# The experts' down projection as three fp32r products instead of one fp32 product, with the operands split by ScalarE and VectorE

## The chip, the cores and the metric

The kernel runs on one core of a Trainium2 chip. The metric is the device time of one execution in microseconds (us), taken as the median of several runs. TensorE does matmuls, transposes and weight loads; VectorE (DVE), ScalarE (ACT) and GpSimd (POOL) do elementwise work; SyncE (SP) only issues DMAs here. Each engine works through its own instructions in order, and semaphores tie the engines together.

## The reference

One layer over 1024 tokens (32 sequences of 32) of width 512, in fp32: `x + cross_attention(layernorm(x))`, then `x + delta_rule_attention(layernorm(x))`, then `x + mixture_of_experts(layernorm(x))`. Only the last part is touched. Every token goes to 2 of 8 experts, and an expert is

```python
gate = jnp.einsum('bted,edf->btef', dispatched, gate_proj)   # 512 -> 1408
up = jnp.einsum('bted,edf->btef', dispatched, up_proj)       # 512 -> 1408
acts = jax.nn.silu(gate) * up
expert_out = jnp.einsum('btef,efd->bted', acts, down_proj)   # 1408 -> 512
```

summed over the two experts with the routing weights.

## The kernel before

The kernel runs its stages one after another. The last, `experts`, works on tokens that `route` has sorted by expert into 23 tiles (`TILES`) of 128 rows. A tile is cut along the 1408 hidden columns into six blocks (`NB`): blocks 0 to 4 are 256 columns wide, block 5 is 128 wide. One step `n` is one block of one tile, so there are 138 steps; `b = n % 6` is the block and `s = n // 6` the tile. "A full block" below is one of 256 columns, "the half block" is block 5.

All weights of the current expert lie in SBUF, gate and up in `w_gu`, down in `w_d`. SyncE reloads them in three groups of two blocks, only where the expert changes (`cond=fresh`), each group once the tile before has done with it. `load_down` waits for that in front of the next loads in the same queue.

What the engines do with a block:

- **The split.** ScalarE copies a block of gate and up weights (128x2048) into fp32r, `gh` (L1495); VectorE subtracts that from the weights and gets the remainder `gl` (L1548). The ring of four buffers lets ScalarE do block n+3 and VectorE block n+2 in step n. The tokens are split likewise once a tile (`xh` L1479, `xl` L1539).
- **gate_up(n)**, TensorE: 12 fp32r matmuls, three products `gh·xh`, `gl·xh`, `gh·xl` for each of four slices (L1437 to L1439), into PSUM.
- **silu** by ScalarE (L1508), times the up half by VectorE, giving `hid` (L1562).
- **turn_h(n)**: TensorE transposes `hid` (L1447), ScalarE copies it from PSUM to `hT` (L1519).
- **down(n)**: TensorE multiplies `hT` with `w_d` in plain fp32 (L1460), one product for each chunk of 128 hidden columns: two chunks in a full block, one in the half block. All 11 chunks of a tile add up in one PSUM bank. ScalarE stores the result at the end (`store_y`, L1485, L1487).

The order on the engines is written out by hand. In step n it is, on TensorE: `gate_up(n)`, `down(n - 2)`, `turn_h(n - 1)`, and `turn_x` for the next tile if `b == 2`. On ScalarE: silu(n); `store_y` of the last tile if `b == 1`; the copy `gh(n + 3)`; the copy `hT(n - 1)`; `take_x` if `b == 2`. On VectorE: hid(n), gl(n + 2), and `split_x` if `b == 2`. `hid`, `silu` and `hT` each have two buffers.

Of the kernel before, what the change touches and what calls it, by code (L numbers as in the profile page):

```python
# [11 lines left out]
F32 = mybir.dt.float32  # L12
F32R = mybir.dt.float32r
U8 = mybir.dt.uint8
I32 = mybir.dt.int32
ALU = mybir.AluOpType
# [3 lines left out]
P = 128  # L20
B, N, C = 32, 32, 512
# [22 lines left out]
BLK = 256  # L44
RING = 4
NB = -(-F // BLK)
# [1303 lines left out]
def experts(nc, d, ps, ident, x_nat, slot, slot_w, tile_expert, out):  # L1350


    with ExitStack() as ctx:
        sb = lambda name, shape, dt=F32: ctx.enter_context(nc.sbuf_tensor(name, shape, dt))
        sem = lambda name: ctx.enter_context(nc.semaphore(name))
        w_gu, w_d = sb("w_gu", [P, KC, 2, F]), sb("w_d", [P, FC, C])
# [2 lines left out]
        gh, gl = ([sb(f"{name}{i}", [P, KC, 2, BLK], F32R) for i in range(RING)] for name in ("gh", "gl"))  # L1359
        silu = [sb(f"silu{i}", [P, BLK]) for i in range(2)]  # L1360
        hid = [sb(f"hid{i}", [P, BLK]) for i in range(2)]
        hT = [sb(f"hT{i}", [P, BLK // P, P]) for i in range(2)]
        y = [sb(f"y{i}", [P, C]) for i in range(2)]
        spare = w_gu[:, :, :, :].rearrange("p k a f -> p (k a f)")
        yg = [[spare[:, (2 * t + r) * C:(2 * t + r + 1) * C] for t in range(NT)] for r in range(2)]
# [11 lines left out]
        with nc.Block() as block:  # L1377
            @block.sync
            def _(sp):
                def load_x(s):  # L1380
                    if s >= 3:
                        sp.wait_ge(x_turned, s - 2)
                    sp.dma_start(xs[s % 3][:, :], d["x_slots"][s * P:(s + 1) * P, :]).then_inc(x_in[s % 3], 16)

                def load_gate_up(s, e, g):
                    if s:
                        sp.wait_ge(gl_done, (s - 1) * NB + 2 * g + 2)
                    cols = group(g)
                    for n, src in enumerate(("gate_proj", "up_proj")):
                        sp.dma_start(w_gu[:, :, n, cols],  # L1390
                                     d[src][bass.ds(e, 1), :, cols].rearrange("a (k p) f -> p (a k) f", p=P), cond=fresh).then_inc(gu_in[g], 16)

                def load_down(s, e, g):
                    if s:
                        sp.wait_ge(d_done, (s - 1) * NB + 2 * g + 2)
                    rows = group(g)
                    sp.dma_start(w_d[:, rows.start // P:rows.stop // P, :],
                                 d["down_proj"][bass.ds(e, 1), rows, :].rearrange("a (c p) n -> p (a c) n", p=P), cond=fresh).then_inc(d_in[g], 16)

                load_x(0)  # L1400
                for s in range(TILES):
                    e = sp.value_load(tile_expert[0:1, 0, s:s + 1], min_val=0, max_val=E - 1)
                    fresh = sp.value_load(tile_expert[0:1, 1, s:s + 1], min_val=0, max_val=1)
                    if s + 1 < TILES:
                        load_x(s + 1)
                    load_gate_up(s, e, 0)
                    load_gate_up(s, e, 1)
                    load_down(s, e, 0)
                    load_gate_up(s, e, 2)
                    load_down(s, e, 1)  # L1410
                    load_down(s, e, 2)
                for t in range(NT):
                    sp.wait_ge(summed, 2 * (t + 1))
                    sp.dma_start(out.rearrange("b n c -> (b n) c")[t * P:(t + 1) * P, :], x_nat[:, t, :]).then_inc(stored, 16)
                sp.wait_ge(stored, 16 * NT)

            @block.tensor
            def _(pe):
                def turn_x(s):
                    pe.wait_ge(x_in[s % 3], 16 * (s // 3 + 1))  # L1420
                    if s:
                        pe.wait_ge(xl_done, s)
                    for k in range(KC):
                        mm = pe.transpose(ps[X_BANK][:, k * P:(k + 1) * P], xs[s % 3][:, k * P:(k + 1) * P], ident[:, :])  # L1424
                    mm.then_inc(x_turned, 1)

                def gate_up(n):
                    s, b, bw = n // NB, n % NB, width(n % NB)
                    if b == 0:
                        pe.wait_ge(xl_done, s + 1)  # L1430
                    pe.wait_ge(gl_done, n + 1)
                    if n >= 3:
                        pe.wait_ge(hid_done, n - 2)
                    bank = ps[GU_BANK + n % 3][:, 0:2 * bw].rearrange("p (a f) -> p a f", a=2)
                    for k in range(KC):
                        hi, lo = gh[n % RING][:, k, :, 0:bw], gl[n % RING][:, k, :, 0:bw]
                        pe.matmul(bank, xh[s % 2][:, k, :], hi, start=(k == 0), stop=False)  # L1437
                        pe.matmul(bank, xh[s % 2][:, k, :], lo, start=False, stop=False)  # L1438
                        mm = pe.matmul(bank, xl[s % 2][:, k, :], hi, start=False, stop=(k == KC - 1))  # L1439
                    mm.then_inc(gu_done, 1)  # L1440

                def turn_h(n):
                    pe.wait_ge(hid_done, n + 1)
                    if n >= 2:
                        pe.wait_ge(hT_done, n - 1)
                    for c in range(width(n % NB) // P):
                        mm = pe.transpose(ps[H_BANK + n % 2][:, c * P:(c + 1) * P], hid[n % 2][:, c * P:(c + 1) * P], ident[:, :])  # L1447
                    mm.then_inc(h_turned, 1)

                def down(n):  # L1450
                    s, b = n // NB, n % NB
                    pe.wait_ge(hT_done, n + 1)
                    if b % 2 == 0:
                        pe.wait_ge(d_in[b // 2], 16 * (s + 1))
                    if b == 0 and s >= 2:
                        pe.wait_ge(y_ready, s - 1)
                    cs = range(width(b) // P)
                    bank = ps[Y_BANK + s % 2]
                    for c in cs:
                        mm = pe.matmul(bank, hT[n % 2][:, c, :], w_d[:, b * (BLK // P) + c, :], start=(b == 0 and c == 0),  # L1460
                                       stop=(b == NB - 1 and c == cs[-1]))
                    mm.then_inc(d_done, 1)

                turn_x(0)
                for n in range(STEPS + 2):
                    if n < STEPS:
                        gate_up(n)
                    if n >= 2:
                        down(n - 2)
                    if 1 <= n <= STEPS:  # L1470
                        turn_h(n - 1)
                    if n % NB == 2 and n // NB + 1 < TILES:
                        turn_x(n // NB + 1)

            @block.scalar
            def _(act):
# [12 lines left out]
                def split_gate_up(n):  # L1489
# [3 lines left out]
                    if n >= RING:  # L1493
                        act.wait_ge(gu_done, n - RING + 1)
                    nc.scalar.copy(gh[n % RING][:, :, :, 0:bw].rearrange("p k a f -> p (k a) f"),  # L1495
                                   w_gu[:, :, :, b * BLK:b * BLK + bw].rearrange("p k a f -> p (k a) f")).then_inc(gh_done, 1)

                split_gate_up(0)
                take_x(0)
                split_gate_up(1)  # L1500
                split_gate_up(2)
                for n in range(STEPS + 2):
                    if n < STEPS:
                        bw = width(n % NB)
                        act.wait_ge(gu_done, n + 1)
                        if n >= 2:
                            act.wait_ge(hid_done, n - 1)
                        nc.scalar.activation(silu[n % 2][:, 0:bw], ps[GU_BANK + n % 3][:, 0:bw], ACT.Silu).then_inc(silu_done, 1)  # L1508
                    if n >= 2 and (n - 2) % NB == NB - 1:
                        store_y((n - 2) // NB)  # L1510
                    if n + 3 < STEPS:
                        split_gate_up(n + 3)
                    if 1 <= n <= STEPS:
                        m = n - 1
                        bw = width(m % NB)
                        act.wait_ge(h_turned, m + 1)
                        if m >= 2:
                            act.wait_ge(d_done, m - 1)
                        nc.scalar.copy(hT[m % 2][:, 0:bw // P, :].rearrange("p c n -> p (c n)"),  # L1519
                                       ps[H_BANK + m % 2][:, 0:bw]).then_inc(hT_done, 1)  # L1520
                    if n % NB == 2 and n // NB + 1 < TILES:
                        take_x(n // NB + 1)

# [12 lines left out]
            def _(dve):  # L1536
# [6 lines left out]
                def split_gate_up(n):  # L1543
                    b, bw = n % NB, width(n % NB)
                    dve.wait_ge(gh_done, n + 1)
                    if n >= RING:
# [3 lines left out]
                                            gh[n % RING][:, :, :, 0:bw].rearrange("p k a f -> p (k a) f").bitcast(F32),  # L1550
                                            ALU.subtract).then_inc(gl_done, 1)

                split_gate_up(0)
                split_x(0)
                split_gate_up(1)
                for n in range(STEPS + 1):
                    if n < STEPS:
                        bw = width(n % NB)
                        dve.wait_ge(silu_done, n + 1)
# [3 lines left out]
                                                ALU.mult).then_inc(hid_done, 1)  # L1563
                    if n + 2 < STEPS:
                        split_gate_up(n + 2)
                    if n % NB == 2 and n // NB + 1 < TILES:
                        split_x(n // NB + 1)
                for t in range(NT):
# [64 lines left out]
```

## Time and profile before

| | |
|---|---|
| median of 3 runs | 2028.21 us (2022.68 to 2029.91) |
| the profiled execution: own time | 2025.16 us |
| the profiled execution: span | 2023.4 us |
| mean granted TensorE clock, as a share of 2.4 GHz | 0.892 |
| TensorE matmul busy | 1584.4 us, 78% |
| VectorE busy | 1183.8 us, 59% |
| ScalarE busy | 707.2 us, 35% |
| the 506 instructions of the down projection (L1460) | 242.2 us of TensorE |

The span is the time from the first to the last instruction; the own time is what the run is counted with. Busy shares are means over stages that have different limits, so they say little about one stage. A matmul's duration runs from its start until its results are through the array; matmuls overlap, so what one costs in a stream is the distance between two starts and not the duration. The same holds, less strongly, for neighbouring instructions of VectorE and ScalarE.

### The profile page before, as it was taken

Reading aid. Unit: us, or ns where it says so; the run is one execution under the profiler, and the core shown is the slowest. Engines: PE = TensorE matmul, PEld = TensorE weight load, DVE = VectorE, ACT = ScalarE, POOL = GpSimd, SP = SyncE. Lnnn points to the kernel's source line nnn. Section 1 sums busy time; section 2 is a strip of 40 time slices with the busy share of each in tenths; the row PEclk is TensorE's granted clock in tenths of the full one; section 3 lists DMA queues with packets and bytes.
Section 4 is the critical chain, followed back from the end, with each engine's and each line's share of the span. In section 5 each row is a group of like instructions: output and inputs, shape, how many; then the busy total and the mean of one; then the engine's idle time right before and its main releaser. Section 6 shows DMA issues by size and latency. Waiting matters only on the chain. (4 is left out here: it accounts for less than half of the span.)

```text
span 2023.4 us, 21832 instructions
## 1 busy us (share of the span) xinstructions
PE 1584.4 (78%) x7119; PEld 1126.2 (56%) x7119; DVE 1183.8 (59%) x2547; ACT 707.2 (35%) x1358; POOL 90.2 (4%) x262
## 2 busy tenths in 40 slices
PE   6999999999599999309600079609999999999993
PEld 3777777777477777203200056406666666666662
DVE  3355545654503888999999733225555555555553
ACT  2333333333234554200000112105555555555550
POOL 0000000000000000002111100030000000000003
PEclk9999999999799999759855579759999999999997
DMA  3111011100125335513000142045435515325004
GB/s 110 33 32 31 16 31 31 31 22 10 39 90 88 71 44 62 88 48 114 0 0 0 41 125 47 1 175 197 161 133 183 176 37 192 130 84 192 22 11 130
DMA packets 116487, 153.31 MB, mean 76 GB/s; under 512 B 47120, under 2 KB 68112, under 8 KB 116400
## 3 DMA queue, kind: packets, MB, share of 16 engines
q1 hardware_dynamic: 110528, 137.81, 23.3%
q0 software_dynamic: 2560, 8.39, 1.3%
q10 hardware_dynamic: 3312, 6.03, 0.8%
q8 instruction: 44, 0.72, 0.2%
q14 instruction: 43, 0.35, 0.1%
HBM read 250.58 MB, written 31.39 MB: 139 GB/s over the span
## 5 line engine op out<-in xcount | busy, mean ns | idle before, releaser
L1548 DVE TENSOR_TENSOR gl<-w_gu,gh 128x2048 fp32r<-128x2048 f32 x138 | 290.8, 2107 | 34.3 <-ACT gh L1495 34.3
L1495 ACT CAST gh<-w_gu 128x2048 fp32r<-128x2048 f32 x138 | 242.4, 1757 | 66.3 <-DMA w_gu<-in_up_proj 56.4
L1460 PE MATMUL bank<-w_d,hT 128*128 128x512 f32 x506 | 242.2, 597 | 9.4 <-ACT hT L1519 9.3
L1437 PE MATMUL bank<-gh,xh 128*128 128x512 f32 (+1 forms) x552 | 219.3, 397 | 11.6 <-DVE xl L1539 11.4
L1562 DVE TENSOR_TENSOR hid<-silu,bank 128x256 f32<-128x256 f32 x138 | 55.1, 399 | 263.6 <-ACT silu L1508 263.5
L1439 PE MATMUL bank<-gh,xl 128*128 128x512 f32 (+1 forms) x552 | 207.4, 376 | 0.0
L1438 PE MATMUL bank<-gl,xh 128*128 128x512 f32 (+1 forms) x552 | 206.5, 374 | 0.0
L1113 PE MATMUL bank<-o_v,o_outw 128*128 128x64 f32 x256 | 36.3, 311 | 182.6 <-DMA o_v<-scratch_v_rows 182.6
L1113 PEld LDWEIGHTS bank<-o_v,o_outw 128*128 128x128 f32 x256 | 36.2, 227 | 186.5 <-DMA o_v<-scratch_v_rows 183.6
L1460 PEld LDWEIGHTS bank<-w_d,hT 128*128 128x128 f32 x506 | 91.6, 188 | 82.8 <-issue 55.2
L939 PE MATMUL bank<-wg,xnT 128*128 128x512 f32 x128 | 61.5, 625 | 88.1 <-DMA bg_row<-in_bg 88.1
L1508 ACT ACTIVATE silu<-bank 128x256 f32<-128x256 f32 x138 | 50.7, 367 | 216.6 <-PE bank L1439 216.6
L1437 PEld LDWEIGHTS bank<-gh,xh 128*128 128x128 f32 x552 | 104.3, 189 | 33.3 <-DVE xl L1539 11.8
L497 DVE COPY probT<-bank 128x512 f32<-128x512 f32 x64 | 41.1, 685 | 134.1 <-PE bank L385 134.1
L1439 PEld LDWEIGHTS bank<-gh,xl 128*128 128x128 f32 x552 | 104.1, 189 | 20.3
L1438 PEld LDWEIGHTS bank<-gl,xh 128*128 128x128 f32 x552 | 104.7, 190 | 15.5
L947 ACT ACTIVATE r_root<-r_nm 128x8 f32<-128x8 f32 x32 | 6.7, 210 | 281.9 <-DVE r_nm L1025 281.9
L939 PEld LDWEIGHTS bank<-wg,xnT 128*128 128x128 f32 x128 | 23.9, 197 | 124.1 <-DMA bg_row<-in_bg 88.3
L449 ACT ACTIVATE prob<-bank,neg_max 128x257 f32<-128x257 f32 x128 | 59.1, 474 | 78.2 <-DVE neg_max L484 78.2
L995 DVE TENSOR_TENSOR r_prod<-r_gram,r_pr 128x512 f32<-128x512 f32 (+23 forms) x158 | 83.8, 549 | 0.0
L436 ACT COPY xv<-bank 128x512 f32<-128x512 f32 x64 | 37.6, 588 | 125.4 <-PE bank L345 125.4
L343 PE MATMUL bank<-xa_wkv_hi,ctx_hi 128*128 128x512 f32 x192 | 78.6, 409 | 0.6 <-PEq L240 0.6
(256 smaller groups left out, 3028.5 us busy)
## 6 DMA issues: line engine op xcount, KB each, us to landing
w_gu<-in_gate_proj SPq DMA_DIRECT2D x46, 1024.0 KB
w_gu<-in_up_proj SPq DMA_DIRECT2D x46, 1024.0 KB
w_d<-in_down_proj SPq DMA_DIRECT2D x46, 1024.0 KB
w_gu<-in_gate_proj SPq DMA_DIRECT2D x23, 768.0 KB
w_gu<-in_up_proj SPq DMA_DIRECT2D x23, 768.0 KB
w_d<-in_down_proj SPq DMA_DIRECT2D x23, 768.0 KB
ctx_raw<-in_ctxT SPq DMA_DIRECT2D x32, 385.5 KB, 3.9
scratch_gram<-gram SPq DMA_DIRECT2D x8, 768.0 KB, 3.3
```

What stands on the lines that cost most here:

```text
L343: pe.matmul(bank, hi(k), other_hi(k), start=(k == 0), stop=False)
L449: nc.scalar.activation(prob[s][:, c, :], ps[c][:, 0:M], ACT.Exp, bias=neg_max[s][:, c:c + 1], accum_out=total[s][:, c:c + 1]).then_inc(exp ...
L939: pe.matmul(ps[n % 8], xnT[:, k, t * P:(t + 1) * P], wg[:, k, hf * 512:(hf + 1) * 512], start=(k == 0), stop=False)
L995: ins = tt(parts[x][:, a], G[:, :, lo:hi, 2, 0:cols], bc(pr[nxt % 2][:, a, :, None, 0:cols], [SG, hi - lo, cols]), ALU.mult)
L1113: mm = pe.matmul(ps[O_BANK + 2 * s + h // 8][:, (h % 8) * DK:(h % 8 + 1) * DK], outw[s][:, h, :], v_row[s][:, h, :], start=True, stop=True)
L1437: pe.matmul(bank, xh[s % 2][:, k, :], hi, start=(k == 0), stop=False)
L1438: pe.matmul(bank, xh[s % 2][:, k, :], lo, start=False, stop=False)
L1439: mm = pe.matmul(bank, xl[s % 2][:, k, :], hi, start=False, stop=(k == KC - 1))
L1460: mm = pe.matmul(bank, hT[n % 2][:, c, :], w_d[:, b * (BLK // P) + c, :], start=(b == 0 and c == 0), stop=(b == NB - 1 and c == cs[-1]))
L1495: nc.scalar.copy(gh[n % RING][:, :, :, 0:bw].rearrange("p k a f -> p (k a) f"), w_gu[:, :, :, b * BLK:b * BLK + bw].rearrange("p k a f -> ...
L1548: nc.vector.tensor_tensor(gl[n % RING][:, :, :, 0:bw].rearrange("p k a f -> p (k a) f"), w_gu[:, :, :, b * BLK:b * BLK + bw].rearrange("p ...
L1562: nc.vector.tensor_tensor(hid[n % 2][:, 0:bw], silu[n % 2][:, 0:bw], ps[GU_BANK + n % 3][:, bw:2 * bw], ALU.mult).then_inc(hid_done, 1)
```

## The change

The down projection becomes three fp32r products like those of gate and up. For a block, `hh` is the fp32r copy of the transposed hidden block and `hl` what remains; `dh` and `dl` are the same for the block of down weights. TensorE then does `hh·dh`, `hh·dl` and `hl·dh` for each chunk. ScalarE makes `hh` (in the place of `hT`) and then `dh`; VectorE makes `hl` and `dl` in step n + 1, behind its other work of that step. Each of the four has two buffers. The wait for the down weights' arrival moves from TensorE to ScalarE, and SyncE's reload of `w_d` waits for `dl` instead of for the down projection. `hT_done` now says that `hh` is there.

```diff
-        hT = [sb(f"hT{i}", [P, BLK // P, P]) for i in range(2)]
+        hh, hl = ([sb(f"{name}{i}", [P, BLK // P, P], F32R) for i in range(2)] for name in ("hh", "hl"))
+        dh, dl = ([sb(f"{name}{i}", [P, BLK // P, C], F32R) for i in range(2)] for name in ("dh", "dl"))
+        hl_done, dh_done, dl_done = sem("hl_done"), sem("dh_done"), sem("dl_done")
...
                 def load_down(s, e, g):
                     if s:
-                        sp.wait_ge(d_done, (s - 1) * NB + 2 * g + 2)
+                        sp.wait_ge(dl_done, (s - 1) * NB + 2 * g + 2)
...
                 def turn_h(n):
                     pe.wait_ge(hid_done, n + 1)
                     if n >= 2:
-                        pe.wait_ge(hT_done, n - 1)
+                        pe.wait_ge(hl_done, n - 1)
...
                 def down(n):
                     s, b = n // NB, n % NB
-                    pe.wait_ge(hT_done, n + 1)
-                    if b % 2 == 0:
-                        pe.wait_ge(d_in[b // 2], 16 * (s + 1))
+                    pe.wait_ge(hl_done, n + 1)
+                    pe.wait_ge(dl_done, n + 1)
...
                     for c in cs:
-                        mm = pe.matmul(bank, hT[n % 2][:, c, :], w_d[:, b * (BLK // P) + c, :], start=(b == 0 and c == 0),
-                                       stop=(b == NB - 1 and c == cs[-1]))
+                        pe.matmul(bank, hh[n % 2][:, c, :], dh[n % 2][:, c, :], start=(b == 0 and c == 0), stop=False)
+                        pe.matmul(bank, hh[n % 2][:, c, :], dl[n % 2][:, c, :], start=False, stop=False)
+                        mm = pe.matmul(bank, hl[n % 2][:, c, :], dh[n % 2][:, c, :], start=False, stop=(b == NB - 1 and c == cs[-1]))
                     mm.then_inc(d_done, 1)
...
+                def split_down(n):                                     # ScalarE
+                    s, b, cs = n // NB, n % NB, width(n % NB) // P
+                    if b % 2 == 0:
+                        act.wait_ge(d_in[b // 2], 16 * (s + 1))
+                    if n >= 2:
+                        act.wait_ge(d_done, n - 1)
+                    nc.scalar.copy(dh[n % 2][:, 0:cs, :], w_d[:, b * (BLK // P):b * (BLK // P) + cs, :]).then_inc(dh_done, 1)
...
-                        nc.scalar.copy(hT[m % 2][:, 0:bw // P, :].rearrange("p c n -> p (c n)"),
+                        nc.scalar.copy(hh[m % 2][:, 0:bw // P, :].rearrange("p c n -> p (c n)"),
                                        ps[H_BANK + m % 2][:, 0:bw]).then_inc(hT_done, 1)
+                        split_down(m)
...
+                def split_down(n):                                     # VectorE
+                    b, cs = n % NB, width(n % NB) // P
+                    if n >= 2:
+                        dve.wait_ge(d_done, n - 1)
+                    dve.wait_ge(hT_done, n + 1)
+                    nc.vector.tensor_tensor(hl[n % 2][:, 0:cs, :].rearrange("p c n -> p (c n)"), ps[H_BANK + n % 2][:, 0:cs * P],
+                                            hh[n % 2][:, 0:cs, :].rearrange("p c n -> p (c n)").bitcast(F32), ALU.subtract).then_inc(hl_done, 1)
+                    dve.wait_ge(dh_done, n + 1)
+                    nc.vector.tensor_tensor(dl[n % 2][:, 0:cs, :], w_d[:, b * (BLK // P):b * (BLK // P) + cs, :],
+                                            dh[n % 2][:, 0:cs, :].bitcast(F32), ALU.subtract).then_inc(dl_done, 1)
...
                 split_gate_up(0)
                 split_x(0)
                 split_gate_up(1)
-                for n in range(STEPS + 1):
+                for n in range(STEPS + 2):
...
                     if n + 2 < STEPS:
                         split_gate_up(n + 2)
+                    if 1 <= n <= STEPS:
+                        split_down(n - 1)
                     if n % NB == 2 and n // NB + 1 < TILES:
                         split_x(n // NB + 1)
```

## Rows read from the trace of the kernel before

**Rows 1.** Windows: length; PE, PEld, DVE, ACT, POOL busy (count); clock, DMA share, GB/s.

```profile
1864.17:1891.14 26.97, 26.63 (x110) 18.14 (x110) 15.23 (x13) 14.91 (x21) 0.00 (x0) 1.00 0.15 55
1390.09:1984.96 594.87, 586.29 (x2396) 398.54 (x2395) 332.15 (x284) 325.05 (x437) 0.00 (x0) 1.00 0.35 121
```

**Rows 2.** Timeline of TensorE over that tile: start, duration, instruction, idle before.

```profile
1864.17 1.98 PE L1460 MATMUL bank<-w_d,hT 128*128 128x512 f32 x4 [0.34 <-ACT hT L1519]
...
1869.41 1.88 PE L1460 MATMUL bank<-w_d,hT 128*128 128x512 f32 x4
1871.13 0.38 PE L1447 MATMUL bank<-ident,hid 128*128 128x128 f32 x2
...
1871.59 0.40 PE L1438 MATMUL bank<-gl,xh 128*128 128x512 f32 x1
...
1874.13 1.88 PE L1460 MATMUL bank<-w_d,hT 128*128 128x512 f32 x4
...
1877.51 1.88 PE L1460 MATMUL bank<-w_d,hT 128*128 128x512 f32 x4
...
1882.21 1.88 PE L1460 MATMUL bank<-w_d,hT 128*128 128x512 f32 x4
...
1886.81 1.02 PE L1460 MATMUL bank<-w_d,hT 128*128 128x512 f32 x2
...
1890.41 0.39 PE L1439 MATMUL bank<-gh,xl 128*128 128x512 f32 x1
1891.14 1.98 PE L1460 MATMUL bank<-w_d,hT 128*128 128x512 f32 x4 [0.34 <-ACT hT L1519]
```

**Rows 3.** Timeline of ScalarE over the same tile.

```profile
1864.29 1.04 ACT L1495 CAST gh<-w_gu 128x1024 fp32r<-128x1024 f32 x1
1866.41 0.37 ACT L1519 COPY hT<-bank 128x256 f32<-128x256 f32 x1 [1.07 <-PE bank L1447]
...
1869.61 0.39 ACT L1508 ACTIVATE silu<-bank 128x256 f32<-128x256 f32 x1 [2.18 <-PE bank L1439]
1869.89 1.90 ACT L1495 CAST gh<-w_gu 128x2048 fp32r<-128x2048 f32 x1
...
1887.86 0.59 ACT L1485 COPY y<-bank 128x512 f32<-128x512 f32 x1 [0.47 <-PE bank L1460]
...
1888.91 1.92 ACT L1495 CAST gh<-w_gu 128x2048 fp32r<-128x2048 f32 x1 [0.45 <-ACT y L1485]
1890.73 0.36 ACT L1519 COPY hT<-bank 128x256 f32<-128x256 f32 x1
```

**Rows 4.** Timeline of VectorE over the same tile.

```profile
1867.46 0.69 DVE L1539 TENSOR_TENSOR xl<-bank,xh 128x512 fp32r<-128x512 f32 x1 [0.41 <-ACT xh L1479]
1870.03 0.42 DVE L1562 TENSOR_TENSOR hid<-silu,bank 128x256 f32<-128x256 f32 x1 [1.87 <-ACT silu L1508]
1870.37 1.22 DVE L1548 TENSOR_TENSOR gl<-w_gu,gh 128x1024 fp32r<-128x1024 f32 x1
...
1875.09 2.28 DVE L1548 TENSOR_TENSOR gl<-w_gu,gh 128x2048 fp32r<-128x2048 f32 x1
```

**Rows 5.** Timeline of ScalarE where the expert has changed.

```profile
1412.16 1.91 ACT L1495 CAST gh<-w_gu 128x2048 fp32r<-128x2048 f32 x1 [2.63 <-DMA w_gu<-in_up_proj]
```

**Rows 6.** Timeline of TensorE at the end of the stage.

```profile
1984.96 1.88 PE L1460 MATMUL bank<-w_d,hT 128*128 128x512 f32 x4
...
1989.97 1.13 PE L1460 MATMUL bank<-w_d,hT 128*128 128x512 f32 x2 [0.35 <-ACT hT L1519]
```

**Rows 7.** Timeline of TensorE before the experts' stage.

```profile
1275.29 1.09 PE L1123 MATMUL bank<-ident,o_g 128*128 128x128 f32 x8 [2.21 <-DVE o_g L1204]
```

**Rows 8.** Windows, busy time and granted clock around it.

```profile
1260.00:1280.00 20.00, 16.34 (x74) 9.81 (x73) 6.57 (x9) 3.82 (x7) 0.00 (x0) 1.00 0.00 0
```

**Rows 9.** Timeline of TensorE in the stage's first step, at the lower clock.

```profile
1366.90 0.63 PE L1438 MATMUL bank<-gl,xh 128*128 128x512 f32 x1
1367.33 0.63 PE L1439 MATMUL bank<-gh,xl 128*128 128x512 f32 x1
```

## The prediction

> **What bounds the kernel now.** I began with the page. Its slices show the experts' stage as the last third of the span, with TensorE at nine tenths or more. Then I measured one tile by windows: 26.97 us, of which TensorE is busy 26.63, VectorE 15.23 and ScalarE 14.91, at full clock [rows 1]. So TensorE sets the pace, and VectorE has 11.7 us a tile to spare and ScalarE 12.1. The shares stop there: they don't say whether new work of those two will be finished in time for TensorE. For that I read the timelines of the three engines over this tile.
>
> The reader should mark in the timeline of TensorE the moments when gate_up(n) is through and down(n-2) may start. I call them E, with the block b of step n as number: E3 = 1869.41, E4 = 1874.13, E5 = 1877.51, E0 = 1882.21, E1 = 1886.81 [rows 2]. In step b=2 the last gate-and-up matmul starts at 1890.41. Such matmuls follow one another every 0.23 us (1871.59 to 1874.13 is 11 of them), so E2 is 1890.64; the down projection starts at 1891.14. That is the one wait of the tile, 0.50 us, and its first weight load then isn't hidden: the group takes 1.98 instead of 1.88 us, 0.10 more [rows 2].
>
> The cause is the useful find. In step b=1 ScalarE stores y before it copies `gh`, so the copy of `hT` comes late: y at E1 + 1.05, `gh` at E1 + 2.10, `hT` at E1 + 3.92, done at E1 + 4.28 [rows 3]. In an ordinary step ScalarE starts silu at E + 0.20 and `gh` at E + 0.48, and a successor starts 0.10 us before the duration ends (1888.91 + 1.92 against 1890.73), so `hT` starts at E + 2.28 [rows 3]. TensorE wants it at the next step's E, over 3 us later in most steps.
>
> **The gain on TensorE.** Two chunks cost 1869.41 to 1871.13, 1.72 us, 0.86 a chunk [rows 2]. Three fp32r products cost 3 x 0.23 = 0.69 a chunk. That saves 0.17 a chunk: 0.34 in a full block, 0.17 in the half one, 11 x 0.17 = 1.87 us a tile. The stretches between the E's without waits, old and new, are: E2 to E3 (with turn_x) 5.14, 4.80; E3 to E4 4.72, 4.38; E4 to E5 3.38, 3.04; E5 to E0 4.70, 4.36; E0 to E1 4.60, 4.26; E1 to E2 (its down projection is the half block) 3.83, 3.66. New sum: 24.50 us.
>
> **The work added.** For a full block: `hh` costs what `hT` does, 0.37. `dh` is 128x1024 on ScalarE, like the half `gh`: 1.04 [rows 3]. `hl` reads PSUM at 256 columns like `hid`: 0.42. `dl` is 128x1024 on VectorE, like the half `gl`: 1.22 [rows 4]. For the half block: `dh` 0.62 (1.04 less 512 columns at the 0.84 ns that two sizes of `gh`, 1.90 and 1.04, give), `hl` 0.29, `dl` 0.69 like `xl` [rows 4]. VectorE rises to 15.23 + 5 x 1.64 + 0.98 = 24.4 us a tile, ScalarE to 14.91 + 5 x 1.04 + 0.62 = 20.7. Both are just under 24.5: by throughput all is hidden. By order it isn't.
>
> The row and the Trainium skill differ here on one price. "VectorE: DVE Perf Modes", section on the TRN2 errata, gives SBUF-source operations 58 cycles beside one per element at 0.96 GHz, so an estimated 1.13 us for `dl`; the row with 1.22 is this very shape. By the page the three large waits below would each shrink by 0.09, some 6 us in all.
>
> **The chain.** down(n-1) now needs `dl(n-1)`, the last thing that VectorE does in step n, behind `hid`, `gl(n+2)` and `hl`, and behind `dh(n-1)`, the last thing of ScalarE in that step. In an ordinary full step: ScalarE has `hh` at E + 2.28, `dh` from E + 2.56 to E + 3.60. VectorE starts `hid` at E + 0.62 and `gl` 0.34 later [rows 3, 4], which leaves it at E + 3.16, and does `hl` until E + 3.50. `dl` waits for `dh`: E + 3.63 to E + 4.85. With 0.05 us until TensorE starts (`hT` 1890.73 + 0.36 to 1891.14), down(n-1) can start at E + 4.90. TensorE gets there at 4.38 or sooner. Step by step through the tile; each line is the step in which `dl` is made, the wait falls at the next E, and 0.10 is for the exposed load at a wait:
>
> - b=0: the half block's `dl` is ready at E0 + 4.1, TensorE comes at 4.26: no wait.
> - b=1: the down projection of three matmuls ends 0.16 earlier, so y starts at E1 + 0.89, `gh` at 1.94, `hh` at 3.76, `dh` 4.04 to 5.08, `dl` 5.11 to 6.33, ready 6.38. TensorE comes at E1 + 3.66. **Wait 2.72**, with the load 2.82.
> - b=2: TensorE is late itself now. turn_h(n-1) starts at E2 + 2.82 + 1.38 = 4.20, and `hh` 0.42 later (1866.41 against a transpose started at about 1865.99, that is 1864.17 + 1.82), so `dl` is ready at 7.24; TensorE comes at 2.82 + 4.80 = 7.62: no wait.
> - b=3: the ordinary case, 4.90 against 4.38: wait 0.52, with load 0.61.
> - b=4: turn_h is later by that 0.61, `hh` at E4 + 2.41, ready at 5.03; TensorE comes at 0.61 + 3.04 = 3.65 (gate_up is the half block): wait 1.38, with load 1.48.
> - b=5: `hh` at E5 + 1.48 + 1.38 + 0.42 = 3.28, ready 5.90; TensorE comes at 5.84: wait 0.06, with load 0.16.
>
> Sum: 5.07 us of waits, a tile of 24.50 + 5.07 = 29.57 us, 2.60 more than 26.97. Over the 22 tile-to-tile periods: **+57.2 us**.
>
> **The rest.** The first tile stores no y. Its ordinary waits cost some 1.2 us more than it saves. At the end nothing covers the chain: today the last gate_up is through at 1984.96 and the last down projection ends at 1991.10, 6.1 later [rows 6]. New, from the same point: wait 1.3 for `dl`, 0.10 + 1.38 until turn_h, 0.42, then 2.62 (`hh` 0.28, `dh` 1.04, `dl` 1.22 and 0.08 between) gives 5.9; again 1.48, 0.3, and 1.6 for the half block gives 9.2; 0.9 of matmuls: 10.1. That is +4.0; the last tile's shorter steps give 0.5 back: **+3.5**. Down weights: ScalarE asks for them some 2 us before TensorE did, and SyncE reloads them about 1.4 us earlier; with a tile between reload and use that moves nothing. Gate and up: at a change of expert ScalarE waits up to 2.63 us for `w_gu` [rows 5], in step b=3. SyncE sends that load behind the wait for the half block's `w_d`, which now ends with its `dl` about 1.1 us earlier, while b=3 comes 4 us later after E1 (3.66 + 7.62 against 3.83 + 0.50 + 5.24 = 9.57, so 1.7, in all 2.8): the wait vanishes. The 22 tiles took 594.87 us, 1.5 more than 22 x 26.97 [rows 1], so **-1.5**, no more.
>
> Sum: 57.2 + 1.2 + 3.5 - 1.5 = +60.4 on 2025.16, so 2085.6. The profiled execution was 3.05 below the median of its runs; I forecast **2088 us**, 3.0% slower.
>
> **The rivals.**
>
> 1. *The forecast, 0.72.* For it: each duration has a row of its own shape, and the 0.50 us wait shows the chain of b=1 at work already.
> 2. *Throughput decides, 0.07.* Waits shrink because what is late in one step is caught up in the next; TensorE's 24.50 then counts beside today's wait of 0.6. 22 x (25.10 - 26.97) = -41, near 1987 us. It wins if the waits sum to under 2.47 us a tile. Against it: `dl` stands behind `gl` in VectorE's order, and nothing lets it pass.
> 3. *Only the y wait is real, 0.07.* If the small instructions run about 0.5 us shorter in sum, b=3 and half of b=4 fall away: 24.50 + 2.82 makes +0.35 a tile, +8, and the end +3: near 2038. Slightly longer b=4 waits lead up to 2060.
> 4. *The clock falls, 0.10.* TensorE would stand idle about 2.5 us in each tile. The longest such gap that I find at full clock is 2.21 us, in a stretch where it was 82% busy and the clock stayed 1.00 [rows 7, 8]; mine would be just longer, at 83% busy. At the lower clock matmuls follow every 0.43 instead of 0.23 us [rows 9]. If the first 8 behind the wait ran so, 22 x 8 x 0.20 = +35: 2123. All 18 of that step: +79, of which later waits would absorb some. The Trainium skill ("TensorE: Matmul & The Clock Gate", Why this matters for your kernels) says likewise that idle gaps between bursts return the clock to half; no row of this case shows it for so short a gap.
> 5. *Other sizes, 0.04,* such as slower copies while DMAs run.
>
> **Range and chances.** An error of 0.2 us in each of three waits is 13 us. That gives 2062 to 2112 about the likeliest; the clock's first case takes the upper end to 2125, and about 2 in 10 stay out. Half a percent, 10 us, is about what a measurement can tell from no change. Faster 0.07; within it 0.05 (part of rival 3); slower 0.88.
>
> **What the profile after would show.** Right: L1460's place taken by 759 matmuls 0.23 us apart; a tile of about 29.6 us, TensorE idle 5 us of it; VectorE near 83% busy and ScalarE 70% in that stage; the wait of the first down matmul put down to VectorE's `dl`, 2.5 to 2.8 us once a tile in front of block 0's down projection, and 1.4 and 0.5 us in front of those of blocks 3 and 2; `dl` waiting for ScalarE's `dh`. Wrong: waits spread evenly or absent, `dl` starting well before E + 3.6, or a granted clock under 1.00 behind the long wait.

## The result, and the profile after

The changed kernel takes 2116.55 us (median of 4 runs, 2115.56 to 2116.89) against 2026.64 for the kernel before in the same runs: a ratio of 1.0444, 95% interval 1.0423 to 1.0464. It is 4.4% slower. The forecast was 2088, the range 2062 to 2125.

The page of the changed kernel, busy shares and the span in 40 slices:

```profile
PE 1578.3 (75%) x7372; PEld 1186.4 (56%) x7372; DVE 1383.2 (65%) x2823; ACT 829.3 (39%) x1496; POOL 89.7 (4%) x262
...
PE   6999999998799995077000796188888888888882
...
PEclk9999999999799998589555797599999999999996
```

TensorE is busy for 6 us less than before and the span is 92 us longer. In the experts' stage its slices read eight where they read nine. VectorE's busy time has grown by 199 us and ScalarE's by 122.

The windows of two tiles, from one store of y to the next. Columns as in [rows 1]:

```profile
1682.22:1713.38 31.16, 26.76 (x123) 21.05 (x121) 23.92 (x26) 20.29 (x26) 0.00 (x0) 0.95 0.06 18
1713.38:1743.24 29.86, 25.43 (x123) 20.08 (x121) 23.83 (x26) 20.28 (x26) 0.00 (x0) 1.00 0.79 282
```

The second of these is a tile at full clock: 29.86 us against 26.97 [rows 1], with VectorE at 80% and ScalarE at 68%. The first takes 1.3 us more, and there the mean granted clock is 0.95. The 21 periods between two stores, the last left out, come in two kinds: nine of 29.80 to 29.87 us and twelve of 31.15 to 31.63.

The timeline of TensorE in the tile at full clock, with the end of the tile before it (the first three rows, where the clock is full again). L1461, L1462, L1463 are `hh·dh`, `hh·dl`, `hl·dh`; only marked starts are shown, to be read as [rows 2] were:

```profile
1703.55 0.47 PE L1461 MATMUL bank<-dh,hh 128*128 128x512 f32 x1 [1.34 <-DVE dl L1572]
...
1708.16 0.47 PE L1461 MATMUL bank<-dh,hh 128*128 128x512 f32 x1
...
1712.49 0.39 PE L1461 MATMUL bank<-dh,hh 128*128 128x512 f32 x1
...
1715.93 0.39 PE L1441 MATMUL bank<-gh,xl 128*128 128x512 f32 x1
1718.91 0.47 PE L1461 MATMUL bank<-dh,hh 128*128 128x512 f32 x1 [2.59 <-issue]
...
1723.80 0.39 PE L1461 MATMUL bank<-dh,hh 128*128 128x512 f32 x1
...
1728.80 0.47 PE L1461 MATMUL bank<-dh,hh 128*128 128x512 f32 x1 [0.49 <-DVE dl L1572]
...
1733.40 0.47 PE L1461 MATMUL bank<-dh,hh 128*128 128x512 f32 x1 [1.34 <-DVE dl L1572]
```

The last gate-and-up matmul of step b=2 starts at 1715.93, so E2 is 1716.16, and the down projection starts at 1718.91: a wait of 2.75 us. From 1723.80 to 1728.80 is the next: down(n-1) starts 5.00 us after E3. The forecast had 4.90. The profile names VectorE's `dl` as the one waited for, except at 1718.91, where it finds nobody; there the next rows show that it was `dl` too.

ScalarE and VectorE in step b=1 of the same tile, to be read as [rows 3, 4] were:

```profile
1713.38 0.59 ACT L1487 COPY y<-bank 128x512 f32<-128x512 f32 x1 [0.31 <-PE bank L1463]
...
1714.43 1.92 ACT L1497 CAST gh<-w_gu 128x2048 fp32r<-128x2048 f32 x1 [0.45 <-ACT y L1487]
1716.24 0.37 ACT L1529 CAST hh<-bank 128x256 fp32r<-128x256 f32 x1
1716.50 1.05 ACT L1506 CAST dh<-w_d 128x1024 fp32r<-128x1024 f32 x1
```

```profile
1716.71 0.42 DVE L1569 TENSOR_TENSOR hl<-bank,hh 128x256 fp32r<-128x256 f32 x1 [0.98 <-ACT hh L1529]
1717.58 1.22 DVE L1572 TENSOR_TENSOR dl<-w_d,dh 128x1024 fp32r<-128x1024 f32 x1 [0.45 <-ACT dh L1506]
```

y, then `gh`, then `hh`, then `dh`, and only then, at 1717.58, VectorE's `dl`, which ends at 1718.80. TensorE starts 0.11 us later. Here is the chain of the forecast, link by link: E1 is 1712.49, so y is at E1 + 0.89 (forecast 0.89), `gh` at 1.94 (1.94), `hh` at 3.75 (3.76), `dh` at 4.01 (4.04), `dl` at 5.09 (5.11) and the down projection at 6.42 (6.38).

The waits over the whole stage: who waited for whom, us in total, times, the longest:

```profile
DVE dl L1572 <- ACT dh L1506: 49.0, 115, 0.5
PE bank L1461 <- DVE dl L1572: 48.6, 48, 2.8
...
ACT gh L1497 <- DMA w_gu<-in_up_proj: 1.2, 1, 1.2
```

`dl` waits for `dh` in 115 of 138 steps, 0.4 us each time: the two helpers work one behind the other. ScalarE's waits for gate and up weights at a change of expert are gone: the one that is left, 1.2 us at 1369.31, belongs to the stage's first loads, and the kernel before has it too (1.24 us at 1366.85).

TensorE behind the long wait in the tile before (1682 to 1713):

```profile
1687.74 0.76 PE L1461 MATMUL bank<-dh,hh 128*128 128x512 f32 x1 [2.57 <-issue]
...
1689.16 0.63 PE L1461 MATMUL bank<-dh,hh 128*128 128x512 f32 x1
...
1690.44 0.50 PE L1449 MATMUL bank<-ident,hid 128*128 128x128 f32 x2
```

The gap was the same, 2.57 us, but here the matmuls take 0.63 to 0.76 instead of 0.39 to 0.47 us, and the two groups of three are 1.42 and 1.28 us apart instead of 0.77 and 0.69. That is the lower clock of rival 4.

### The profile page after: what moved, and what is told of

The parts are those of the page before. It is cut to its first block and busy times, and to the rows that moved or that the text cites. A ratio compares the mean times of both kernels' runs of the same rounds, so it can differ in the third digit from the quotient of the medians.

```text
span 2115.1 us, 23025 instructions
## 1 busy us (share of the span) xinstructions
PE 1578.3 (75%) x7372; PEld 1186.4 (56%) x7372; DVE 1383.2 (65%) x2823; ACT 829.3 (39%) x1496; POOL 89.7 (4%) x262
## 5 line engine op out<-in xcount | busy, mean ns | idle before, releaser
L1439 PE MATMUL bank<-gh,xh 128*128 128x512 f32 (+1 forms) x552 | 219.3, 397 | 12.8 <-DVE xl L1550 12.6
L1461 PE MATMUL bank<-dh,hh 128*128 128x512 f32 x253 | 113.2, 447 | 104.9 <-issue 54.3
L1572 DVE TENSOR_TENSOR dl<-w_d,dh 128x1024 fp32r<-128x1024 f32 x138 | 156.6, 1135 | 49.0 <-ACT dh L1506 49.0
L1506 ACT CAST dh<-w_d 128x1024 fp32r<-128x1024 f32 x138 | 135.6, 983 | 0.0
L1461 PEld LDWEIGHTS bank<-dh,hh 128*128 128x128 f32 x253 | 50.4, 199 | 144.1 <-issue 134.5
L1463 PE MATMUL bank<-dh,hl 128*128 128x512 f32 x253 | 106.3, 420 | 0.0
L1462 PE MATMUL bank<-dl,hh 128*128 128x512 f32 x253 | 105.7, 418 | 0.0
L1569 DVE TENSOR_TENSOR hl<-bank,hh 128x256 fp32r<-128x256 f32 x138 | 55.2, 400 | 61.1 <-ACT hh L1529 58.9
```

The source lines that it names most:

```text
L1461: pe.matmul(bank, hh[n % 2][:, c, :], dh[n % 2][:, c, :], start=(b == 0 and c == 0), stop=False)
L1462: pe.matmul(bank, hh[n % 2][:, c, :], dl[n % 2][:, c, :], start=False, stop=False)
L1463: mm = pe.matmul(bank, hl[n % 2][:, c, :], dh[n % 2][:, c, :], start=False, stop=(b == NB - 1 and c == cs[-1]))
L1506: nc.scalar.copy(dh[n % 2][:, 0:cs, :], w_d[:, b * (BLK // P):b * (BLK // P) + cs, :]).then_inc(dh_done, 1)
L1572: nc.vector.tensor_tensor(dl[n % 2][:, 0:cs, :], w_d[:, b * (BLK // P):b * (BLK // P) + cs, :], dh[n % 2][:, 0:cs, :].bitcast(F32), ALU.su ...
```

## The experiments

Times are medians, each with the ratio to the kernel before on the same chip. The rows come from different chips, on which the kernel before took 2024.97 to 2027.25 us, so differences of a few us between rows are better read from the ratios. A tile is the period between two stores of y in the profile.

| run | us | ratio, 95% interval | tile, us |
|---|---|---|---|
| the change | 2116.55 | 1.0444 (1.0423 to 1.0464) | 29.86 or 31.4 |
| filler matmuls in the long wait | 2095.07 | 1.0331 (1.0314 to 1.0348) | 29.85 |
| store of y late | 2073.82 | 1.0233 (1.0216 to 1.0250) | 28.40 |
| `dh`, `dl` a step earlier | 2010.21 | 0.9913 (0.9897 to 0.9930) | 26.28 |
| both of these | 1986.44 | 0.9800 (0.9784 to 0.9817) | 25.22 |
| down weights split only twice | 2012.42 | 0.9930 (0.9913 to 0.9946) | 26.28 |
| kernel before, store late | 2017.07 | 0.9952 (0.9936 to 0.9969) | 26.35 |
| both, `hh`/`hl` first in block 4 | 2008.11 | 0.9911 (0.9894 to 0.9927) | 26.27 |
| both, old condition for the reload | 2012.68 | 0.9943 (0.9924 to 0.9962) | 25.23, seven of 28.0 to 32.5 |
| the change, old condition for the reload | 2113.58 | 1.0438 (1.0421 to 1.0456) | 29.84 or 31.4, one 32.9 |

**Is it the clock that makes 12 of 21 tiles longer?**

```diff
                     if n < STEPS:
                         gate_up(n)
+                    if n % NB == 2 and n >= NB:
+                        for _ in range(8):
+                            pe.matmul(ps[X_BANK], xh[(n // NB) % 2][:, 0, :], gh[n % RING][:, 0, :, 0:BLK], start=True, stop=True)
                     if n >= 2:
                         down(n - 2)
```

> The changed kernel, and in every tile but the first TensorE does 8 needless fp32r matmuls into a PSUM bank that is free at that moment, in front of block 0's down projection, where it stands idle for 2.6 us; they take 8 x 0.23 = 1.84 us. In the changed kernel's trace 8 of the 22 periods between two stores of y take 29.8 to 29.9 us at full clock and 14 take 31.2 to 31.6 us, with the lower clock behind that wait. Theory A (the clock falls because of the idle stretch and costs the 1.5 us in these 14 tiles and at the end): all periods become 29.8 to 29.9 us, granted clock 1.00 in the stage, time down by 15 x 1.5 = 22 us to about 2094. Theory B (the longer tiles come from something else, such as loads of weights or late engines, and the lower clock only goes with it): the periods stay mixed and the time stays at 2115 to 2118. Theory C (the filler matmuls get in the way): above 2120.

(The counts in it are off: it is nine and twelve, and the last, longer period beside them.) Measured: 2095.07, as theory A said. TensorE around the fillers (L1472), and the window of 100 us, whose clock is now 1.00:

```profile
1736.27 1.98 PE L1472 MATMUL bank<-gh,xh 128*128 128x512 f32 x8
1739.00 0.47 PE L1461 MATMUL bank<-dh,hh 128*128 128x512 f32 x1 [0.76 <-issue]
1739.31 0.40 PE L1462 MATMUL bank<-dl,hh 128*128 128x512 f32 x1
```

```profile
1700.00:1800.00 100.00, 91.43 (x429) 72.42 (x428) 79.53 (x84) 67.50 (x88) 0.00 (x0) 1.00 0.36 123
```

All of the 21 periods but two are 29.8 to 29.9 us. In one of the two (30.55) the expert changes and ScalarE waits 0.63 us for `w_gu`; in the other (30.12) it doesn't change, and ScalarE's `gh` starts 0.28 us later behind y than in the other tiles. TensorE did 176 needless matmuls and the kernel became 21.5 us faster: what twelve longer tiles at 1.5 us and the longer end at 2.4 us had cost. So rival 4 is real, and it is one of two causes, not the only one: without it the kernel is still 3.3% slower than before.

**Is the long wait the store of y?**

```diff
-                    if n >= 2 and (n - 2) % NB == NB - 1:
-                        store_y((n - 2) // NB)
...
                     if n % NB == 2 and n // NB + 1 < TILES:
                         take_x(n // NB + 1)
+                    if n >= 2 and (n - 2) % NB == NB - 1:
+                        store_y((n - 2) // NB)
```

> The changed kernel, with ScalarE's store of y moved from behind silu to the end of its step; nothing else. Theory A (the long wait in front of block 0's down projection is the store in front of gh, hh and dh, and the clock falls only because of that wait): that wait goes from 2.6 to about 1.2 us, a tile takes 29.85 - 1.5 = 28.3 us, the clock stays at 1.00, time 2116 - 22 x 1.5 - 22 = 2061, range 2050 to 2070. Theory B (the chain of an ordinary step is all that matters and the store is beside the point): no shorter than 2105. Theory C (waits move: what block 0 gains is lost by block 1, whose copies now run behind the store): 2085 to 2100 with the clock at 1.00.

Measured 2073.82, tile 28.40, at full clock. The wait is 1.13 us where 1.2 was expected. The mechanism is theory A's, the time 13 us above it and beyond its range. The periods tell most of it: seven of them, those in which the expert changes, take 28.8 to 31.5 us, 10 us more than seven of 28.40. There ScalarE waits for `w_gu`, 1.60 us in this one, and TensorE in turn, 2.19 us, with the lower clock behind it (the matmul takes 0.67). So the clock didn't stay at 1.00 either: it fell in two of the seven.

```profile
1558.70 1.91 ACT L1497 CAST gh<-w_gu 128x2048 fp32r<-128x2048 f32 x1 [1.60 <-DMA w_gu<-in_up_proj]
```

```profile
1551.63 0.47 PE L1461 MATMUL bank<-dh,hh 128*128 128x512 f32 x1 [1.13 <-issue]
...
1563.22 0.67 PE L1461 MATMUL bank<-dh,hh 128*128 128x512 f32 x1 [2.19 <-DVE dl L1572]
...
1569.22 0.47 PE L1461 MATMUL bank<-dh,hh 128*128 128x512 f32 x1 [1.17 <-DVE dl L1572]
```

So the long wait had been giving the loads their time: with it ScalarE waits for `w_gu` at no change of expert, without it at all seven. I had not thought of that in the expectation, though the prediction counts it.

**Order or amount?**

```diff
-        dh, dl = ([sb(f"{name}{i}", [P, BLK // P, C], F32R) for i in range(2)] for name in ("dh", "dl"))
+        dh, dl = ([sb(f"{name}{i}", [P, BLK // P, C], F32R) for i in range(3)] for name in ("dh", "dl"))
...
-                        split_down(m)
+                    if n < STEPS:
+                        split_down(n)
...
                     if 1 <= n <= STEPS:
-                        split_down(n - 1)
+                        split_hidden(n - 1)
+                    if n < STEPS:
+                        split_down(n)
```

VectorE's `split_down` is cut in two (`split_hidden` makes `hl`), and `d_done` is asked for one step less strictly for `dh` and `dl`.

> The changed kernel, with dh and dl made one step earlier (three buffers each): in step n ScalarE makes dh(n) and VectorE dl(n), behind hh(n-1) and hl(n-1). The work of each engine is unchanged; only what down(n-1) waits for gets shorter, ending with hl(n-1). The store of y stays where it was. Theory A (order, not amount, costs the time): the waits in front of blocks 2, 3 and 4 vanish, the one of block 0 goes from 2.6 to about 1.0 us, a tile takes 24.5 + 1.1 = 25.6 us, time 2026 - 22 x 1.4 = 1996, range 1985 to 2010, faster than the kernel before. Theory B (the amount costs it: VectorE with 24.4 us a tile and ScalarE with 20.7 can't keep up, since each waits for the other): 2030 or more, with VectorE over 90% busy.

Measured 2010.21, tile 26.28 where theory A said 25.6: faster than the kernel before, just above the range that theory A gave. Theory B is out: the same work, on the same engines, costs 106 us less where TensorE doesn't wait for it, the clock's part included. Two waits are left in a tile:

```profile
1723.52 0.50 PE L1461 MATMUL bank<-dh,hh 128*128 128x512 f32 x1 [0.85 <-DVE hl L1570]
...
1736.42 0.50 PE L1461 MATMUL bank<-dh,hh 128*128 128x512 f32 x1 [0.45 <-DVE hl L1570]
```

0.85 in front of block 0 was expected as 1.0. The other, 0.45 in front of block 3, was not: I had written that it would vanish. `hl` stands behind `gl` in VectorE's order and is ready some 3.6 us after E4, while the next gate_up is the half block and takes TensorE there in 3.04.

> The changed kernel without the repeated split of the down weights: dh and dl are made for the first two blocks only and used for all later ones, so the down projection is computed with the wrong weights from block 2 on. TensorE does the same 759 matmuls; ScalarE is spared dh (5 x 1.05 + 0.63 us a tile), VectorE dl (5 x 1.22 + 0.68). What down(n-1) waits for ends with hl(n-1), as in the run with dh and dl one step earlier, whose tile took 26.28 us. Theory A (order): dh and dl cost nothing once they are not what TensorE waits for, so this kernel's tile takes the same 26.1 to 26.4 us and the time is 2005 to 2014. Theory B (amount): freed of a quarter of their work the engines are faster than in that run, a tile of 25.5 us or less, below 1998.

```diff
-                        split_down(m)
+                        if m < 2:
+                            split_down(m)
...
+                    if n >= 2:
+                        return
                     dve.wait_ge(dh_done, n + 1)
...
-                    pe.wait_ge(dl_done, n + 1)
+                    pe.wait_ge(dl_done, min(n, 1) + 1)
```

(The wait for `d_in` goes back to TensorE and the reload's condition to `d_done`.) Measured 2012.42, tile 26.28:

```profile
1700.00:1726.30 26.30, 25.00 (x123) 20.26 (x122) 17.25 (x20) 15.04 (x21) 0.00 (x0) 1.00 0.08 26
```

The same window of the run with `dh` and `dl` a step earlier:

```profile
1719.72:1746.01 26.29, 24.99 (x123) 20.24 (x121) 23.51 (x26) 20.13 (x27) 0.00 (x0) 1.00 0.12 34
```

VectorE does 17.25 instead of 23.51 us of work in that time, ScalarE 15.04 instead of 20.13, and the ordinary tile isn't 0.01 us shorter. The split of the down weights costs nothing once it is off the path. The tiles are the fair comparison here and not the times: with the old condition for the reload ScalarE waits for `w_gu` at all seven changes of expert, up to 2.55 us, and in the other run at none.

**Both edits, and the fair comparison.**

> Both of the last two edits: dh and dl one step earlier, and the store of y at the end of ScalarE's step. Theory A: no wait is left on TensorE but small ones, a tile takes 24.5 to 25.0 us, time 2026 - 22 x 2.2 = 1978, range 1968 to 1990. Theory B (VectorE's 24.4 us a tile is now the bound): a tile takes 25.5 us or more, 1995 to 2010, VectorE over 95% busy and TensorE waiting for hl or gl in every step.

> The kernel before, with only the store of y moved to the end of ScalarE's step. Theory A (the one wait of its tile, 0.50 us and 0.10 for the exposed weight load, is the store in front of gh and hT): tile 26.97 - 0.60 = 26.37 us, time 2027 - 13 = 2014, range 2011 to 2018. Theory B (that wait comes from hT's own chain whatever the store does): 2025 or more.

Measured 1986.44 and 2017.07, both within theory A's ranges; the tile of the first lies between the two theories, though, at 25.22 us. The first is the fastest version found: 2.0% faster than the kernel before, 1.5% faster than the kernel before with the same late store. Its tile, and the one wait of it that the timeline shows:

```profile
1733.00:1758.24 25.24, 24.77 (x122) 20.23 (x120) 23.57 (x26) 19.86 (x28) 0.00 (x0) 1.00 0.88 313
```

```profile
1746.05 0.50 PE L1461 MATMUL bank<-dh,hh 128*128 128x512 f32 x1 [0.47 <-DVE hl L1570]
```

VectorE is busy 23.57 of 25.24 us, 93%, and TensorE 98%. 24.50 us of matmuls by the forecast and 0.47 + 0.10 for this wait make 25.07 of the 25.22. The kernel before with the late store has lost its 0.60 a tile (26.35, expected 26.37), but five of its tiles take 27.3 to 28.0 us, where the expert changes.

> The fastest run so far (dh and dl one step earlier, store at the end of the step; tile 25.22 us), and in steps of block 4 alone hh(n-1) comes before gh(n+3) on ScalarE and hl(n-1) before gl(n+2) on VectorE. The next gate_up is the half block there, so TensorE comes after 3.04 us, while hl, behind gl, is ready after 3.6. Theory A: that last wait (0.47 us and 0.10) vanishes, tile 24.6 to 24.8 us, time 1986 - 11 = 1975, range 1970 to 1980. Theory B (the copies and splits pushed back, gh(1) and gl(0) of the next tile, are late in turn): no gain, 1984 to 1995, with waits of gate_up for gl.

```diff
-                    if n + 3 < STEPS:
+                    if n + 3 < STEPS and n % NB != 4:
                         split_gate_up(n + 3)
...
                                        ps[H_BANK + m % 2][:, 0:bw]).then_inc(hT_done, 1)
+                    if n + 3 < STEPS and n % NB == 4:
+                        split_gate_up(n + 3)
...
-                    if n + 2 < STEPS:
+                    if n + 2 < STEPS and n % NB != 4:
                         split_gate_up(n + 2)
                     if 1 <= n <= STEPS:
                         split_hidden(n - 1)
+                    if n + 2 < STEPS and n % NB == 4:
+                        split_gate_up(n + 2)
```

Measured 2008.11, tile 26.27, 1.05 longer. Theory A fell, and B only half holds: the time is 13 us above its range too. The wait for `hl` in front of block 3 is gone, and two others have come: a small one of gate_up for `gl` (0.20), and 1.04 for the next `hl`:

```profile
1708.90 0.47 PE L1439 MATMUL bank<-gh,xh 128*128 128x512 f32 x1 [0.20 <-issue]
...
1712.94 0.50 PE L1461 MATMUL bank<-dh,hh 128*128 128x512 f32 x1 [1.04 <-DVE hl L1572]
```

```profile
1708.93 1.23 DVE L1580 TENSOR_TENSOR dl<-w_d,dh 128x1024 fp32r<-128x1024 f32 x1
...
1710.27 2.29 DVE L1562 TENSOR_TENSOR gl<-w_gu,gh 128x2048 fp32r<-128x2048 f32 x1
1712.47 0.42 DVE L1572 TENSOR_TENSOR hl<-bank,hh 128x256 fp32r<-128x256 f32 x1
```

`gl` and `dl` now run until 1710.2, so `hid`, the next `gl` and `hl` of the short step b=5 are late by as much. A VectorE that is 93% busy has no room for a reorder that leaves it waiting: here it waited 1.22 us for `hh` first.

**When may the weights be reloaded?**

```diff
-                        sp.wait_ge(dl_done, (s - 1) * NB + 2 * g + 2)
+                        sp.wait_ge(d_done, (s - 1) * NB + 2 * g + 2)
```

> The fastest run so far (dh and dl one step earlier, store at the end of the step; every tile 25.2 us, those where the expert changes too), with one condition put back as the kernel before had it: SyncE reloads a group of w_d when its down projection is done, not when dl is. Gate and up weights stand behind that wait in SyncE's queue. Theory A (the early release is what keeps changes of expert free there; the kernel before with only the store moved has the old condition and 27.3 to 28.0 us instead of 26.35 in six of its tiles): the loads come 2 to 4 us later, up to seven tiles take 1 to 3 us longer, time 1986 + 10 = 1996, range 1991 to 2005. Theory B (loads are hidden anyway): 1984 to 1989 and no tile longer than 25.4 us.

> The changed kernel with the same one condition put back. The prediction gave the change 1.5 us for ScalarE's vanished wait for gate and up weights, 1.1 us of it from the earlier reload and 1.7 us from block 3's later place behind the store. Theory A (the long wait in front of block 0 hides the loads even with the old condition): no difference, 2113 to 2119. Theory B (the early reload is needed here too): changes of expert cost ScalarE a wait of about 1 us, tiles get longer by as much, 2119 to 2125.

Measured 2012.68 and 2113.58. In the fastest version the one line is worth 26 us (29 by the ratios), more than twice what theory A said and beyond its range: seven tiles take 28.0 to 32.5 us (of the kernel named in the expectation it is five tiles, not six). ScalarE at the first change of expert in it, then in the fastest version at the same place, then TensorE in the former:

```profile
1413.02 1.90 ACT L1497 CAST gh<-w_gu 128x2048 fp32r<-128x2048 f32 x1 [3.91 <-DMA w_gu<-in_up_proj]
```

```profile
1410.70 1.91 ACT L1497 CAST gh<-w_gu 128x2048 fp32r<-128x2048 f32 x1
```

```profile
1415.77 0.50 PE L1461 MATMUL bank<-dh,hh 128*128 128x512 f32 x1 [2.73 <-DVE hl L1570]
...
1420.38 0.50 PE L1461 MATMUL bank<-dh,hh 128*128 128x512 f32 x1 [1.29 <-DVE hl L1570]
```

One wait of 3.91 us makes TensorE wait 2.73 and 1.29. In the changed kernel the same line is worth nothing (2113.58 against 2116.55, whose ratios' intervals overlap), as theory A said: there the loads are hidden by the long wait, and ScalarE waits for `w_gu` at no change of expert. The one period of 32.9 us is the clock's: around it the granted clock stays down twice as long as in the other tiles (it was 0.53 from 1528 to 1532 us and 0.81 from 1532 to 1540).

## Why the prediction was right, and where it was too small

The direction, the mechanism and the place of each wait held; the size was 28 us short. That the time lies in the range is due to the room left for rival 4: without it the range ended at 2112. So two things happened at once. The chain of the forecast is there, and by itself it gives 2095.07 us (the run with fillers, which keeps the clock up), 7 above the forecast and well inside the narrow range. On top of it came the lower clock behind the long wait, which the prediction itself had listed among the signs that it was wrong. Rival 4's figure, 2123, is nearer than 2088, but partly by luck: the clock cost 20 us and not 35, and the rest was 8 us more than forecast.

- **The gain on TensorE**, 0.34 us a full block: right. Two chunks now take 1723.80 to 1725.16, 1.36 us instead of 1.72. In the fastest version, where it isn't lost again, 25.07 of the tile's 25.22 us are accounted for with it. Rival 2, throughput alone, would have needed the order of that version.
- **The waits.** Forecast 2.72, 0.52, 1.38, 0.06 us; in the rows shown 2.75, 0.65, 1.50, 0.15 (the last at 1708.16, against 1708.01). The ordinary chain is 5.00 and not 4.90 us long, and nearly all of that is the last link: `dl` ends 4.85 us after E3, as forecast (1728.65), but TensorE starts 0.15 us after it and not 0.05. Elsewhere in these rows it is 0.11 to 0.14. Summed, a tile of 29.86 against 29.57. Over the 21 periods between stores: 21 x 2.88 = 60.5 where the forecast's 2.60 gives 54.6.
- **The store of y**, shown by the run that only moves it: the wait, as the profile counts it, goes from 2.57 to 1.13 us. The same store cost the kernel before 0.6 us a tile, shown by its own run.
- **The first tile and the end.** To the first store the stage takes 2.9 us more (forecast 1.2). The last period takes 6.8 more in the run with fillers (29.13 against 22.33), forecast 2.6 + 3.5 = 6.1.
- **The loads**, -1.5: right in size, since no wait for `w_gu` lengthens a tile any more (-2.0). Of the two reasons given only one was needed: the old condition makes no difference to this kernel. In the fastest version the other is the whole thing.
- **The clock** is the step that was mis-sized. I gave it a chance of 0.10, left it out of the sum, and priced it at 35 us or more, or none, as if it would happen in every tile or never. It happened in 12 of 21 tiles and in the last, longer period, at 1.5 us each in the tiles, where the first case had 1.6: 17.9 us between the stores and 2.4 at the end, 20.3 in all; the fillers gave 21.5 back.
- The rest of the difference is 2.5 us by which the profiled execution comes later to its first matmul of the stage, half of it ahead of the stage and half in the first load. The wait in front of that matmul is 12.6 us here and 11.4 before, and in the variants 11.3 to 13.2 without a pattern, so I take it for the spread of single executions.

Together: 2.5 + 2.9 + 60.5 + 17.9 - 2.0 + 9.2 = 91.0 of the 91.7 us between the two spans. The forecast also added 3.05 us because the kernel before was profiled below its median; the changed kernel's runs lie within 1.3 us of each other, so nothing answers to that term.

The sentence on the Trainium skill's clock gate ("TensorE: Matmul & The Clock Gate", Why this matters for your kernels), that idle gaps between bursts return the clock to half, agrees with 13 of the changed kernel's 22 long waits and not with the other nine. The price of 58 cycles (the Trainium skill, "VectorE: DVE Perf Modes", section on the TRN2 errata) is not borne out: `dl` took 1.23 us, no less than the row of before, and the measurement decides. The prediction read that section too narrowly: below its table it says that the 58 are too few, and for fp32 `tensor_tensor` it gives (N + 151) / 0.96 ns, an estimated 1.22 us for `dl`, which agrees with the rows.

## What to carry to other kernels

Work handed to engines with time to spare isn't free because their busy shares fit: add up what must happen between the moment an input exists and the moment the bound engine needs it, in the order in which each helper does it, and put the parts that don't depend on that input (here the split of the weights) a step earlier. That alone turned 4.4% slower into 0.9% faster, and 2.0% with the store moved. When a buffer's reader changes from a late engine to an early one, look at who else is queued behind its release: one condition on SyncE was worth nothing in one order and 26 to 29 us in the other.

## What was not expected of the hardware

- The same gap of TensorE was followed by the lower clock in one tile and by the full clock in the next. Of the 22 long waits of the changed kernel's execution nine, of 2.57 to 2.59 us, kept the full clock; 13 did not, ten of them 2.57 us long and the others 2.60, 2.65 and 2.85. With the old condition for the reload it was 14 of 22. In neither execution did two tiles in a row keep the full clock.
- The fall can come after the gap. With the store moved, TensorE resumed at 1623.56 us after a gap of 2.65 us, at first at full clock (0.47 us for the matmul), and 1.2 us later ran at the lower one:

```profile
1624.79 0.63 PE L1463 MATMUL bank<-dh,hl 128*128 128x512 f32 x1
```

- The length of the gap alone didn't decide it between 2.1 and 3.0 us. In the fastest version with the old condition for the reload gaps of 2.73 us (the row at 1415.77 above) and 3.02 us were followed by the full clock (1.00 in the windows 1413 to 1422 and 1468 to 1478 us), and one of 2.09 us by the lower clock, 1.3 us after its end. With the store moved, one of 2.19 us was too (the row at 1563.22 above), while a gap of 2.21 us stood at full clock in [rows 7, 8]. For a forecast the price has to be taken as a share of the tiles, here 12 of 21, times 1.5 us. What does decide stays open.
- TensorE doing 176 useless matmuls in its idle time made the kernel 1.0% faster.
